# Moving the feed-forward products and two residual sums from VectorE to ScalarE and GpSimd, with weights transposed by the host

## The reference

```python
x = x + 0.5 * ffn(layernorm(x))
x = x + attn(layernorm(x))
x = x + 0.5 * ffn(layernorm(x))

def ffn(x):                        # weights are int32, scaled by 1/127
    h = silu(x @ w_gate.T) * (x @ w_up.T)      # 256 -> 768
    return h @ w_down.T                        # 768 -> 256

def attn(x):                       # a selective scan, N = 16 states, R = 64
    z = x @ W_z.T
    params = x @ W_params.T        # dt part (R), unused part (N), C (N)
    dt = softplus(params[:R] @ W_dt.T + b_dt)
    u = silu(causal_conv(x, conv_w))           # 4 taps, per channel
    A = -exp(A_log); A_tilde = exp(dt * A); B_tilde = (A_tilde - 1) / A
    h[t] = A_tilde[t-1] * h[t-1] + B_tilde[t-1] * u[t-1]
    y = sum_n C[n] * h[n] + u * D
    return (y * silu(z)) @ W_out.T
```

## Time and profile before

| | |
|---|---|
| median of 3 runs | 2673.05 us (2661.23 to 2675.84) |
| the profiled execution, its own time | 2672.35 us |
| its span | 2670.6 us |
| busy: TensorE, VectorE, ScalarE, GpSimd | 2313.0, 2440.3, 1818.3, 1689.3 us |
| mean granted clock of TensorE, share of full speed | 0.93 |

### The profile page before, as it was taken

The page is one execution under the profiler, slowest core; times in us unless marked ns, Lnnn a source line. Parts: engine busy times, 40 slices in busy tenths (PEclk is TensorE's granted clock), DMA queues, the critical chain, the costliest instruction groups (busy, mean ns, idle before and its releaser), DMA issues.

```text
span 2670.6 us, 28167 instructions
## 1 busy us (share of the span) xinstructions
PE 2313.0 (87%) x9268; PEld 1386.2 (52%) x9268; DVE 2440.3 (91%) x2644; ACT 1818.3 (68%) x2499; POOL 1689.3 (63%) x966
## 2 busy tenths in 40 slices
PE   4876889898998989899898989989898998987577
PEld 3533445545554555555555555655555455554345
DVE  3179999999999999999999999999999999999982
ACT  2466778586777868676876868687686858766532
POOL 0147767576676757576675767667576766768650
PEclk8987899999999999999999999999999999998689
DMA  2124333433333333433433343433334333333420
GB/s 62 41 69 144 112 120 109 136 112 134 119 126 120 111 134 119 136 126 111 142 112 127 111 142 112 134 128 119 119 111 142 111 129 126 118 117 110 144 102 16
DMA packets 112279, 307.97 MB, mean 115 GB/s; under 512 B 10913, under 2 KB 45826, under 8 KB 112130
## 3 DMA queue, kind: packets, MB, share of 16 engines
q1 hardware_dynamic: 112130, 306.15, 33.7%
HBM read 288.28 MB, written 17.83 MB: 115 GB/s over the span
## 4 chain that ended last, share of the span: by engine, by line
PE 46%; DVE 26%; issue 15%; ACT 9%; POOL 1%; DMA 1%; SPq 0%; DVEq 0%; POOLq 0%; ACTq 0%
PE work L543 16%; PE work L533 12%; DVE ring L982 10%; DVE g_bank L951 9%; PE work L579 7%; ACT normed L623 4%; PE work L515 3%; PE work L571 2%; ACT ring L737 2%; DVE hid L911 2%; DVE stats L892 2%; PE work L560 2%; PE work L553 1%; DVE acc L939 1%; DMA ring<-c_rows 1%
## 5 line engine op out<-in xcount | busy, mean ns | idle before, releaser
L790 POOL TENSOR_TENSOR acc<-acc,ring 128x1024 f32<-128x1024 f32 x512 | 1204.8, 2353 | 625.2 <-DVE ring L982 619.8
L951 DVE TENSOR_TENSOR_SCAN g_bank<-du_bank,ring 128x1024 f32<-128x1024 f32 x512 | 1175.4, 2296 | 17.0 <-ACT du_bank L726 4.5
L543 PE MATMUL work<-wd_t,hid 128*128 128x256 f32 x3072 | 685.5, 382 | 20.1 <-DVE hid L911 19.7
L982 DVE SCALAR_TENSOR_TENSOR ring<-g_bank,inv_a,ring 128x1024 f32<-128x1024 f32 x512 | 653.8, 1277 | 5.8
L543 PEld LDWEIGHTS work<-wd_t,hid 128*128 128x128 f32 x3072 | 587.5, 192 | 113.2 <-DVE hid L911 22.5
L737 ACT ACTIVATE ring<-dt,a_coef 128x1024 f32<-128x1024 f32 x512 | 548.1, 1138 | 13.3 <-DVE g_bank L951 12.1
L657 ACT ACTIVATE sil<-work 128x512 f32<-128x512 f32 x384 | 220.6, 597 | 261.5 <-PE work L533 260.6
L533 PE MATMUL work<-xt_hi,wg_t 128*128 128x512 f16 x768 | 315.6, 411 | 62.0 <-ACT xt L635 30.5
L911 DVE SCALAR_TENSOR_TENSOR hid<-sil,work 128x512 f32<-128x512 f32 x384 | 259.2, 675 | 95.2 <-PE work L533 95.1
L610 ACT ACT_TABLE_LOAD x257 | 329.7, 1283 | 4.6
L533 PE MATMUL work<-xt_hi,wu_t 128*128 128x512 f16 x768 | 305.6, 398 | 17.7 <-DVE hid L911 13.1
(11 more groups left out here) (93 smaller groups left out, 2492.5 us busy)
## 6 DMA issues: line engine op xcount, KB each, us to landing
ring<-c_rows SPq DMA_DIRECT2D x512, 512.0 KB, 3.6
x_in<-L_attn_x SPq DMA_DIRECT2D x32, 512.0 KB, 4.8
out<-x_fin SPq DMA_DIRECT2D x32, 512.0 KB, 5.3
c_rows<-params SPq DMA_DIRECT2D x32, 32.0 KB, 3.1
ring<-L_ffn_w_gate SPq DMA_DIRECT2D x1, 768.0 KB
ring<-L_ffn_w_up SPq DMA_DIRECT2D x1, 768.0 KB
ring<-L_ffn_w_down SPq DMA_DIRECT2D x1, 768.0 KB
ring<-L_attn_W_z SPq DMA_DIRECT2D x1, 256.0 KB
```

The lines of the kernel that those rows point to most:

```text
L543: last = pe.matmul(dst[:, j * E:(j + 1) * E], hid[:, K.unit["sh", f, bt, c, m] % HIDS, t:t + P], wd_t[:, m, :], start=(m == 0), stop=(m == ...
L790: nc.gpsimd.tensor_tensor(acc[bt % 2][:, h, :], acc[bt % 2][:, h, :], cg[:, slot, :], ALU.add).then_inc(S["summed"], 1)
L951: scan = nc.vector.tensor_tensor_scan(g_bank[:], du_bank[:], decay[:, a, :], 0.0, ALU.add, ALU.mult)
L982: nc.vector.scalar_tensor_tensor(cg[:, k, :], g_bank[:], inv_a[:, h, s:s + 1], spread[:, k_c, :], ALU.mult, ALU.mult).then_inc(S["weighted ...
```

## The change

Three things are done. First, all 24 products of a batch (`sh`) are split: ScalarE copies the `up` bank, scaled, into `hid` (new event `sc`, L672 of the changed kernel), and GpSimd multiplies it in place with the silu (`hp`, L814). Second, the residual sums `rs` of f = 1 and `ra` are split the same way: ScalarE copies the bank (`rs` on ScalarE, L680; `rc`, L687), GpSimd adds in place (`rp`, L821; `ra`, L828). `rs` of f = 2 stays on VectorE (L935). Third, the host hands seven weight matrices over transposed, so that the setup's transposes and copies go; ScalarE converts the int32 weights and makes `tap_diag`, between its first events of the first batch, and each consumer waits for what it needs. All three tables have new numbers.

The core of the diff:

```diff
@@ schedule(), Counts
-                at(t + LAG["up"][0] + LAG["sh"][0], "sh", f, b, c, m)
+                at(t + LAG["up"][0] + LAG["sc"][0], "sc", f, b, c, m)
+                at(t + LAG["up"][0] + LAG["hp"][0], "hp", f, b, c, m)
...
                 after(t0, f"dn{f}", f"rs{f}", 2 * c + jp, "rs", f, b, c, jp)
+                if f == 1:
+                    after(t0, f"dn{f}", "rp1", 2 * c + jp, "rp", b, c, jp)
...
             put(t0, "op", jp, "op", b, jp)
+            after(t0, "op", "rc", jp, "rc", b, jp)
             after(t0, "op", "ra", jp, "ra", b, jp)
...
-    "gu1": 0.816, "gu2": 1.116,
+    "gu1": 0.719, "gu2": 1.107,
...
-        return ({"ga": "si", "up": "sh", "dn": "rs", "op": "ra", "z": "zs", "pm": "pe", "cv": "us", "dt": "da",
+        return ({"ga": "si", "up": "sc", "dn": "rs", "op": "rc", "z": "zs", "pm": "pe", "cv": "us", "dt": "da",
@@ block.sync
+            sp.dma_start(a_coef[:], A_log.rearrange("(h p) n -> p h n", p=P)).then_inc(a_landed, 16)
+            load(0, 0)
+            sp.dma_start(st_g, w_gate.rearrange("(k p) m -> p k m", p=P)).then_inc(g_landed, 16)
+            sp.dma_start(st_u, w_up.rearrange("(k p) m -> p k m", p=P)).then_inc(u_landed, 16)
+            load(0, 1)
...
-                    wait(sp, "free", ("dn", 1, bt - 1, c, 1))
+                        wait(sp, "mid_added", ("rp", bt - 1, c, 1))
@@ block.scalar
-            act.wait_ge(w_landed, 16 * 11)
+            act.wait_ge(a_landed, 16)
             nc.scalar.activation(a_coef[:], a_coef[:], ACT.Exp).then_inc(s_exp, 1)
-            act.wait_ge(w_kept, groups)
-            act.wait_ge(s_set, 1)
...
+                    if (f, bt, c) == (1, 0, 0):
+                        for dst, src, landed in ((wg_t, st_g, g_landed), (wu_t, st_u, u_landed)):
+                            act.wait_ge(landed, 16)
+                            nc.scalar.activation(dst[:], src, ACT.Copy).then_inc(s_cast, 1)
...
-                        wait(act, "free", ("up",) + before[-SILUS][1:])
+                        was = before[-SILUS][1:]
+                        wait(act, "product", ("hp",) + was)
...
+                elif kind == "sc":
+                    job = ("up",) + ev[1:]
+                    wait(act, "ready", job)
+
+                    if ev in K.was:
+                        wait(act, "ready", K.was[ev])
+                    nc.scalar.activation(hid[:, K.unit[ev[1:]] % HIDS, :], bank(job)[:], ACT.Copy,
+                                         scale=H_SCALE).then_inc(freed(job), 1)
+                elif kind == "rs" and ev[1] == 1:
+                    _, f, bt, c, jp = ev
+                    job = ("dn",) + ev[1:]
...
+                    wait(act, "ready", job)
+                    wait(act, "fin_added", ("ra", bt - 2, 2 * c + jp))
+                    nc.scalar.activation(x_mid[bt % 2][:, t, :].rearrange("p j e -> p (j e)"), bank(job)[:], ACT.Copy,
+                                         scale=OUT_SCALE).then_inc(freed(job), 1)
@@ block.gpsimd
-            pool.wait_ge(w_kept, groups)
-            pool.wait_ge(s_set, 1)
+            pool.wait_ge(s_pads, 1)
...
+                elif kind == "hp":
+                    _, f, bt, c, m = ev
+
+                    v = hid[:, K.unit[ev[1:]] % HIDS, :]
+                    wait(pool, "free", ("up",) + ev[1:])
+                    wait(pool, "free", ("ga",) + ev[1:])
+                    k = K.at["silu", ("si",) + ev[1:]][1] % SILUS
+                    nc.gpsimd.tensor_tensor(v, v, sil[:, k, :], ALU.mult).then_inc(S["product"], 1)
...
+                    nc.gpsimd.tensor_tensor(v, v, x_in[:, t, :].rearrange("p j e -> p (j e)"),
+                                            ALU.add).then_inc(S["mid_added"], 1)
...
+                    nc.gpsimd.tensor_tensor(v, v, x_mid[bt % 2][:, t, :].rearrange("p j e -> p (j e)"),
+                                            ALU.add).then_inc(S["fin_added"], 1)
@@ block.vector
-            dve.wait_ge(w_landed, 16 * 11)
-            for w in (st_g, st_u, st_d):
-                then(nc.vector.tensor_copy(w, w.bitcast(I32)))
...
-                        nc.vector.scalar_tensor_tensor(hid[:, i, :], sil[:, K.at["silu", silu][1] % SILUS, :], H_SCALE,
-                                                       bank(job)[:], ALU.mult, ALU.mult).then_inc(freed(job), 1)
...
-                elif kind == "ra":
...
-                            x_mid[bt % 2][:, t, :].rearrange("p j e -> p (j e)"), ALU.add).then_inc(freed(job), 1)
```

More of the change, by code:

```diff
@@ L399, in freed @@
             return free[K.bank[job]]
-        groups = 8 + 3 + 1 + 1 + 1 + 1 + 1
+        LANDED = 16 * 9
         block = ctx.enter_context(nc.Block())
@@ L537, in _ @@
                     _, f, bt, c, jp = ev
-                    wait(pe, "free", ("up", f, bt, c, HM - 1))
+                    hold(pe, s_cast, 3)
+                    wait(pe, "product", ("hp", f, bt, c, HM - 1))
                     dst = take(ev)
@@ L836, in _ @@
             then(nc.vector.tensor_tensor(inv_a[:], inv_a[:], kept[:], ALU.mult))
-            then(nc.vector.tensor_copy(inv_a_u[:, :, C_ROW:C_ROW + N], inv_a[:]))
+            nc.vector.tensor_copy(inv_a_u[:, :, C_ROW:C_ROW + N], inv_a[:]).then_inc(s_inv, 1)
+            dve.wait_ge(s_inv, 1)
             then(nc.vector.tensor_tensor(inv_a[:], inv_a[:], tiny[:], ALU.add))
-            nc.vector.tensor_copy(flag_f[:], ones[0:1, :]).then_inc(s_set, 1)
-            n = 0
-            def keep(copies):
-                nonlocal n
-                dve.wait_ge(w_turned, n + 1)
-                for dst, src in copies(work[n % BANKS]):
-                    last = nc.vector.tensor_copy(dst, src)
-                last.then_inc(w_kept, 1)
-                n += 1
@@ L902, in program @@
                                                        ALU.mult, ALU.mult).then_inc(S["shift"], 1)
-                    elif kind == "sh":
-                        job, silu = ("up",) + ev[1:], ("si",) + ev[1:]
-                        wait(dve, "ready", job)
-                        wait(dve, "free", ("ga",) + ev[1:])
-                        i = K.unit[ev] % HIDS
-                        if ev in K.was:
-                            wait(dve, "ready", K.was[ev])
-                        nc.vector.scalar_tensor_tensor(hid[:, i, :], sil[:, K.at["silu", silu][1] % SILUS, :], H_SCALE,
-                                                       bank(job)[:], ALU.mult, ALU.mult).then_inc(freed(job), 1)
-                    elif kind == "rs":
+                    elif kind == "rs" and ev[1] == 2:
                         _, f, bt, c, jp = ev
```

188 lines of the change are left out of this document (93 added, 95 removed), and 26 rows, old and new, of tables (AT, LAG).

## The result

Twenty runs of the changed kernel have a median of 2671.2 us (2669.9 to 2676.7), twenty of the kernel before one of 2663.06. The ratio of the means is 1.0022, 95% interval 1.0012 to 1.0032: **no change within 0.5%, where 2550 us was forecast.** That outcome had a chance of 0.06 in the forecast, and 2671 lies above its range of 8 in 10 (2488 to 2640). Of the twenty executions before, fourteen lie at 2661 to 2664 us and six, the profiled one among them, at 2671 to 2676, so a difference of 13 us (0.9 us a batch) between single executions can be chance. The profiled spans are 2670.5 us after and 2670.6 before.

What follows compares the result with a forecast made beforehand. VectorE was taken to bound the middle batches, GpSimd after the change. From 2672.35 us: setup -24.6, run-up +5, first batch -10.7, middle -87.5, last batch -9, tail +5 give 2550.6, said as 2550; 8-in-10 range 2488 to 2640.

Steps and rivals of the forecast that it cites:

- Setup: Start to first statistics: a shorter chain takes 12.5 us in place of 37.1, 24.6 less; bounds 18 and 28.
- The run-up's +5: Batch 0 before its first scan: split products and sums lengthen it, with uncovered ScalarE conversions, by 5 us (0 to 12).
- SyncE's queue: Loads of x wait for GpSimd, spreads of C queue behind: costed at nothing, up to 2 us a batch without slack.
- Rival 1: Middle batches: buffers suffice and waits vanish, so a batch takes 144 us and the whole 2495; chance 0.15.
- all 87.5 us: Fourteen middle batches: each falls 6.25 us, from 154.25 to 148, set by GpSimd plus waits; bounds 143 and 154.
- won outside the middle: All stretches but the middle batches: 39 us won, so the whole is as slow as before at 157 us a batch.
- First batch: First batch's slots: with VectorE at 128.7 and GpSimd at 117.1 us busy, 141.7 becomes 131, 10.7 less.
- last batch: Last batch's slots: VectorE's bare 117 us bound it, so 120 in place of 128.9, 9 less.
- The tail: Stretch after the last batch's slots: as in the run-up, 5 us more.
- Rival 3: Middle batches: half of rival 2's waits plus TensorE's banks freed late, 151 to 156 a batch, 2592 to 2662 us; chance 0.17.
- Rival 2: Middle batches: GpSimd stands in ScalarE's queue, over 13 us lost a batch, slower than before, 2718 at 160; chance 0.08.
- Rival 4: Middle batches: VectorE and GpSimd conflict at the shared SBUF port, 153 us a batch, 2620 us; chance 0.05.

Runs made afterwards that it cites:

- e1: Kernel before with only the new setup; all products and sums on VectorE, old tables: 2655.1 us, ratio 0.9928, 153.90 us a batch.
- section 5: Runs on the order of before with the new setup, cutting or adding work on single engines or a pair, and a list of the kernel before's waits: 147.07 to 165.07 us a batch.
- u2: Kernel before with new setup, VectorE's products at half the columns, nothing added: 2644.3 us, 153.91 us a batch.
- v2: Kernel before with new setup, down projection cut to 4 of 6 steps and VectorE's products at half the columns: 2531.0 us, 147.07 us a batch.
- u4: Kernel before with new setup, two spare 256-column copies on ScalarE behind each silu: 2707.1 us, 158.27 us a batch.
- u3: Kernel before with new setup, two spare 256-column products on GpSimd behind each of its additions: 2827.3 us, 165.07 us a batch.
- section 2: Four runs of the changed kernel, each with work cut from one engine: GpSimd 156.19, VectorE 156.21, ScalarE 154.86, TensorE 153.93 us a batch.
- t4: Changed kernel with ScalarE's silu and copy at half the columns and the down projection cut to 4 of 6 steps: 2572.2 us, 150.08 us a batch.
- t1: Kernel before with new setup, a third of the products split to ScalarE and GpSimd, sums on VectorE: 2699.7 us, ratio 1.0097, 157.21 us a batch.
- s4: Changed kernel with VectorE's weighting on 640 of 1024 columns: 2661.38 us, 156.21 us a batch.
- e2: New setup and new tables, but all products and sums on VectorE as before: 3059.3 us, ratio 1.1435, 183.12 us a batch.
- s1: Changed kernel with GpSimd's products on 256 of 512 columns: 2662.31 us, 156.19 us a batch.
- u1: Changed kernel with ScalarE's silu and copy and GpSimd's products at half the columns, down projection cut to 4 of 6 steps: 2494.5 us, 145.22 us a batch.

## Why the prediction was wrong

*Right.* **Setup:** 12.62 us against 12.5. That closeness is luck, since two of its terms were off and cancel: A_log was used at 3.04 us already, and the stand before the first statistics was 6.48 us where 3.64 was taken over.

```profile
3.04 0.18 DVE L876 TENSOR_SCALAR tiny<-a_coef 128x32 f32<-128x32 f32 x1 [0.39 <-ACT a_coef L597]
...
12.62 1.08 DVE L918 BATCH_NORM_STATS2 stats<-x_in 128x6 f32<-128x256 f32 x3 [6.48 <-issue]
```

The run-up's +5 was +5.95, but not for the reason given: e1, which splits nothing, has +4.7 of it. That leaves 1.3 us for the copies and products on that path, to which most of the +5 was put down. Busy times: GpSimd 144.2 against 143.4, ScalarE 129.7 against 132.4. The new product took 1.275 us, the upper bound (1.28), not 1.18, but a queue of them moves on every 1.23 us. SyncE's queue cost nothing, as said: no spread of C is among VectorE's waits in four middle batches.

*The step that failed* is the sentence "The batch cannot come down by 21.6 us; it comes down to where GpSimd stands, plus what the engines lose by waiting for each other", and under it "VectorE bounds the middle, the others wait on it". The loss by waiting was counted between VectorE and GpSimd alone; TensorE and ScalarE came in with their busy times of 141 and 132 us, as if the 13 and more us that they lack were free. Two signs stood in the rows. VectorE's small idle time in the middle was mostly waiting for TensorE (L911, 6.8 us in the four batches of section 5; all but 0.1 of its 95.2 us in the earlier trace rows). Rival 1 said of it that VectorE waited "for engines with 27% and more to spare", but TensorE, busy 141.1 of 153.6 us, had 8%. And TensorE led the chain with 46%. What the runs showed in its place:

- Before the change TensorE, with its waits for ScalarE, was already a second bound at 154 us. u2 removes 7 us a batch from VectorE and gets nothing; only with TensorE shortened too (v2) does the batch move. So VectorE's relief, from which all 87.5 us were to come, was worth close to zero in that order.
- The additions were not free beside it. 16 us a batch on ScalarE, which nobody waits for, cost 4.4 us (u4), GpSimd's 45 us cost 11.2 (u3). The changed kernel has more work on both, and a new order. That the order absorbs most of the cost and leaves +2.2 us is argued, not shown.
- The additions also stand in TensorE's own loop, since its bank comes free after ScalarE's copy and its down projection starts after copy and product. That ScalarE and TensorE together now form the slowest loop is what section 2 (1.6 and 2.5 us, the largest two) and t4 (6.4 for the pair) show.
- In eight middle batches TensorE's mean granted clock is 0.94 of full speed after and 0.95 before, and its busy time 0.8 us a batch more. How much of the +2.2 us that is, or whether it only follows from the longer waits, no run separates.

How much the new order by itself absorbs stays open: no run has all products moved in the order of before. The nearest is t1, with a third of them, which takes 3.3 us a batch more than e1.

VectorE came to 139.2 us and not 128.9. Each removed product had held its queue for 0.59 us rather than 0.675, since it overlapped with its neighbours, which is 2 us a batch; and `shift` (L927) went from 0.28 to 1.04 us on average, +4.6 a batch. Most of the rest is that scans and weightings, as long as before, overlap with their neighbours by 1.9 us a batch less. This didn't decide: 12 us off VectorE gave 0.2 (s4).

*The rest of the sum.* First batch -2.3 for -10.7 and last batch -4.9 for -9; the same step is the likely reason, but no run looked at these alone. The tail came out at -4.85 for +5, where the forecast took the split's latency as a loss. Its gain is the new tables': e2, with these tables and no split, has a tail of 76.0 us, the changed kernel 76.45, and e1, with the tables of before, 81.2.

*The rivals.* By the forecast's own terms 34 us were won outside the middle and not 39, so the point at which the middle eats all of it is 156.7 us a batch and not 157; measured were 156.43, with 30.6 us won outside. Rival 3 named the right place (TensorE's banks freed late, "TensorE at 141 speaks for it"), but gave 151 to 156 a batch and a chance of 0.17. Rival 2 had its signs partly: GpSimd waited for the `hid` copy 5 us a batch, not 13. Rival 1 falls. Rival 4's mechanism is there, but small: L947 took 0.985 us (1.014 before) and GpSimd's additions 2.372 (2.353); only `shift` grew, a VectorE operation with two SBUF inputs. Where it starts beside a running GpSimd instruction, it ends with that instruction. Here the product of 1572.13 ends at 1573.39, and `shift` at 1573.41 (GpSimd, then VectorE):

```profile
1572.13 1.26 POOL L814 TENSOR_TENSOR hid<-hid,sil 128x512 f32<-128x512 f32 x1
1573.36 2.36 POOL L845 TENSOR_TENSOR acc<-acc,ring 128x1024 f32<-128x1024 f32 x1
```
```profile
1572.19 1.22 DVE L927 SCALAR_TENSOR_TENSOR shift<-meanvar,rstd 128x4 f32<-128x4 f32 x1 [2.86 <-POOL rstd L795]
```

Of its 96 instances 75 start beside a running GpSimd instruction in the changed kernel and 17 before, and each of these ends within 0.03 us of that instruction's end. Its median was 0.15 us before and 1.22 after, and 0.68 in s1, where GpSimd's product takes 0.73 us in place of 1.275. The Trainium skill's rule ("SBUF — State Buffer", "Who interferes with whom") agrees with this: such a VectorE instruction and a GpSimd instruction that reads SBUF exclude one another for a whole instruction. The load alone does not tell it: the mean was 0.28, 0.61 and 1.04 us as GpSimd's load rose from 68% to 91% (u3) and 92% of a batch, so 0.61 and 1.04 at nearly one load show that placing counts too.

## What to carry to other kernels

Before you move work off the busiest engine, shorten just that work and leave everything else (half the columns, half of the result left out): if the time doesn't move, as in u2, something else is tied to it, and the move alone will not pay. An engine that is busy 141 of 154 us in a fixed order may have no slack at all; test pairs, since 0.0 and 1.0 alone were 6.8 together. And price a change's independent parts first: here the setup alone was faster than before (0.7% in its own comparison), and the large part gave all of that back.

## What had not been expected of the hardware

- A VectorE operation on four columns (`shift`, L927) with two SBUF inputs took 1.04 us on average beside a nearly always busy GpSimd, 0.28 before. It ended with the GpSimd instruction that it had started beside, up to 2.09 us later.
- GpSimd's in-place product of 128x512 takes 1.275 us, 8% over half of the 1024-column addition (2.372); at 256 columns (u1) it is 0.732 us, so an estimated 0.19 us (2 x 0.732 - 1.275) don't shrink with the columns.
- The table loads (L610 before, L603 after) stayed at 257, though ScalarE got 32 copies more a batch among its decays.
